# A store issued ahead of two transposing transfers of the same tile, on one queue (a four-layer graph network)

## The chip, the cores and the metric

One core of a Trainium2 chip. The metric is the device time of one execution in microseconds (us); most executions of a kernel agree within 0.3%.

## The reference, cut to what is computed

Nodes `x` (6250 x 128, float32), 206,250 edges sorted by target, and four layers, each fed with `relu(layernorm(x))` and added to `x`:

```python
h = relu(layernorm(x))
x = x + segment_sum(edge_weight[:, None] * (sigmoid(h @ W_gate + b_gate) * (h @ W0))[dst], src)   # layer 0
h = relu(layernorm(x))
x = x + segment_sum(h[src], dst) @ W1.T + b1                                                       # layer 1
# layer 2: messages from [h[src], h[dst]], summed by target, with a linear update
# layer 3: a hypergraph layer: sums over edges by one end, scaled by 1/degree, then by the other end,
#          scaled, then a normalisation over all nodes and a relu
```

## The kernel before, in words

The sums over edges are done as matrix products. The nodes are cut into 49 tiles of 128 (`TILES`). A stage called the build makes, for each tile j of source nodes, three matrices of 128 x 6272 (49 blocks of 128 columns, float16, 1.6 MB each): the counts of edges, and the edge weights in a high and a low part. All three stand in `stage[:, b, 0..2]`, with b = j % 2: there are two such buffers.

In the build, per tile:

- VectorE makes one-hot codes (`hots`, lines 788 to 791), eight sets a tile, in two buffers, and adds finished sums to X (`add_four`, line 803).
- TensorE multiplies them into PSUM (`half_windows`, lines 531 to 533: 16 units a tile), takes the high part off the exact sum (`take_high`, line 514), and makes the sums of layer 0 for the tile two back (`sums`, `sum_four`, lines 506 to 508): behind each of the first seven one-hot sets of tile j come up to eight blocks of tile j - 2, 24 matmuls. These read `wt[:, b]`, the turned weights. Before the first of them (line 539) it waits for both turned halves of that tile.
- ScalarE copies PSUM into `stage`: counts and high part together (line 1033, 16 a tile), the low part two units later (line 1016, 16 a tile). At the first unit of tile j, behind a low part of the tile before, it waits for the store (line 1026) and for both transposes (line 1027) of tile j - 2, whose buffer it is going to write.
- SyncE's queue hands each tile on (`hand_on`, lines 325 to 339). It waits until the sums of tile j - 2 are made (329) and until the tile's counts and high parts are copied (332, `hi_done`), loads half of the tile's rows for the sums (`g_in`, 333, 32 KB), issues the transposing transfer of the high part from `stage` to `wt` (334); then the same for the low part; then it stores the counts to DRAM (`by_source`, 336). Tile 0 also stores a filler (339).

`tiles_loop` unrolls seven tiles and then loops seven times over six tiles. After the build four phases read the counts back: phases 1 to 3 as they are (`a_pairs`, 366), phase 4 turned (`a_turned`, 356), and multiply them with the nodes' features (line 578). Before phase 1 all stores must have landed (`counts_stored`), and all additions be made (343).

Of the kernel before, what the change touches and what calls it, by code (L numbers as in the profile page):

```python
# [19 lines left out]
P = 128  # L20
NODES, EDGES = 6250, 206250
TILES = -(-NODES // P)
# [40 lines left out]
def slab(t, j):  # L63

    if isinstance(j, int):
        return t[j]
    return t[bass.ds(j, 1)].rearrange("a p n -> (a p) n")
# [7 lines left out]
def later(j, n):  # L75

    return not isinstance(j, int) or j >= n
# [46 lines left out]
def gnn_kernel(nc, x, src, dst, edge_weight, w0, wg0, bg0, w1, b1, wm, bm, wu, bu, hyper, w3, b3, gamma, beta, out):  # L124
    ctx = ExitStack()
    with ctx:
        sems = {}

        def s(name):
            if name not in sems:  # L130
                sems[name] = ctx.enter_context(nc.semaphore(name))
            return sems[name]
# [3 lines left out]
        def at(name, shape, dt, offset):  # L136
            size = int(np.prod(shape[1:])) * ESIZE[dt]
            return nc.alloc_sbuf_tensor_at(name, shape, dt, offset=offset), offset + -(-size // 32) * 32

        def keep(name, shape, dt):  # L140
            t, place[0] = at(name, shape, dt, place[0])
            return t
# [6 lines left out]
        by_source = nc.dram_tensor("counts_by_source", (TILES, P, (TILES + 1) * P), F16).ap()  # L149
# [14 lines left out]
        cols = keep("cols", [P, 8], F32)  # L164
# [22 lines left out]
        stage, o = at("stage", [P, 2, 1 + WEIGHTS, TILES, P], F16, o)  # L187
# [73 lines left out]
        def vec(ap):  # L261
            return ap.rearrange("(a b) -> a b", a=1)
# [23 lines left out]
        @block.sync  # L286
        def _(sp):

            for a, b in ((dst, dst_pad), (src, src_pad), (edge_weight.bitcast(I32), w_pad)):
                sp.dma_start(b[0:EDGES].rearrange("(a b) -> a b", a=15), a.rearrange("(a b) -> a b", a=15)).then_inc(s("pad_in"), 16)  # L290
            sp.wait_ge(s("pads"), 2)
            for k, b in ((1, dst_pad), (0, src_pad), (0, w_pad)):
                sp.dma_start(vec(b[EDGES:PADDED]), pad_rows[0:1, k, :]).then_inc(s("pad_in"), 16)

            sp.dma_start(X[:, 0:TILES - 1, :], x[0:(TILES - 1) * P].rearrange("(i p) f -> p i f", p=P)).then_inc(s("x_in"), 16)
            sp.wait_ge(s("x_zero"), 1)
            sp.dma_start(X[0:LAST, TILES - 1, :], x[(TILES - 1) * P:NODES]).then_inc(s("x_in"), 16)

            for to, of in ((w0g[:, 0:P], w0), (w0g[:, P:P + 1], wg0), (w3s[:], w3), (w_h[:, 0], wu[0:P]),
                           (wraw[:, 0], w1), (wraw[:, 1], wm[0:P]), (wraw[:, 2], wm[P:2 * P]), (wraw[:, 3], wu[P:2 * P]),  # L300
                           (b1s[:], spread(b1, P)), (bus[:], spread(bu, P)), (cols[:, 4:5], spread(bg0, 1)),
                           (cols[:, 0:1], bm.rearrange("(a b) -> a b", b=1)), (cols[:, 1:2], b3.rearrange("(a b) -> a b", b=1)),
                           (cols[:, 2:3], gamma.rearrange("(a b) -> a b", b=1)), (cols[:, 3:4], beta.rearrange("(a b) -> a b", b=1))):
                sp.dma_start(to, of).then_inc(s("weights_in"), 16)
            sp.wait_ge(s("x_zero"), 2)
            sp.dma_start(hrows[0:TILES - 1, :], hyper[0:(TILES - 1) * P].rearrange("(i p) -> i p", p=P)).then_inc(s("weights_in"), 16)
            sp.dma_start(hrows[TILES - 1:TILES, 0:LAST], vec(hyper[(TILES - 1) * P:NODES])).then_inc(s("weights_in"), 16)

            sp.wait_ge(s("pad_in"), 96)
            sp.dma_start(dst_run[:], bass.AP(dst_pad.tensor, 0, [[RUN, P], [1, RUN + 1]])).then_inc(s("dst_in"), 16)  # L310
            sp.dma_start(w_run[:], bass.AP(w_pad.tensor, 0, [[RUN, P], [1, RUN]])).then_inc(s("w_in"), 16)
            for k, b in enumerate((src_pad, dst_pad, w_pad)):
                sp.dma_start(table[:, k * P:(k + 1) * P], bass.AP(b.tensor, 0, [[ALIGN, ROWS], [1, P]])).then_inc(s("table_in"), 16)  # L313

            def layers(general):
                if general:
                    for ph in range(5):
                        general_sum(ph)
                    return

                sp.wait_ge(s("g_parts"), SET)
                sp.dma_start(g_dram.rearrange("i p n -> p i n"), G[:].rearrange("p i a f -> p i (a f)")).then_inc(s("g_stored"), 16)
                sp.wait_ge(s("g_stored"), 16)

                def hand_on(j, k, c):

                    b = c % 2
                    if later(j, 2):
                        sp.wait_ge(s("four_done"), (j - 1) * FOURS)
                    for a, done in enumerate(("hi_done", "lo_done")):  # L330
                        part = slice(a * P, (a + 1) * P)
                        sp.wait_ge(s(done), (j + 1) * HALVES)
                        sp.dma_start(g_in[:, b, part], slab(g_dram, j)[:, part]).then_inc(s(f"g_loaded{b}"), 16)
                        sp.dma_start_transpose(wt[:, b, a], stage[:, b, 1 + a].rearrange("p i d -> p (i d)")).then_inc(s(f"wt_in{b}"), 16)  # L334
                    cols = slice(j * P, (j + 1) * P) if isinstance(j, int) else bass.ds(j * P, P)
                    sp.dma_start(by_source.rearrange("i p n -> p i n")[:, :, cols], stage[:, b, 0]).then_inc(s(f"stored{b}"), 16)
                    if isinstance(j, int) and j == 0:

                        sp.dma_start(by_source.rearrange("i p n -> p i n")[:, :, TILES * P:], stage[:, b, 0]).then_inc(s("filled"), 16)

                tiles_loop(sp, hand_on, 0)
                counts_stored(sp)
                sp.wait_ge(s("added"), FOURS * TILES)

                for ph in (1, 2, 3, 4):

                    def step(j, k, c, ph=ph):
                        if not on(j):
                            return
                        if ph == 4:  # L350
                            if later(j, SLOTS):

                                sp.wait_ge(s("sum_done4"), j - (SLOTS - 1))
                            else:
                                sp.wait_ge(s("sum_done3"), min(TILES, 46 + c // 2 * 2))
                            sp.dma_start_transpose(a_turned[:, c % SLOTS], slab(by_source, j)[:, 0:TILES * P]).then_inc(s(f"turned_in{c % SLOTS}"), 16)  # L356
                        elif c % 2 == 0:
                            if later(j, SLOTS):

                                sp.wait_ge(s(f"sum_done{ph}"), j - (SLOTS - 2))  # L360
                            elif ph > 1:
                                sp.wait_ge(s(f"sum_done{ph - 1}"), min(TILES, 46 + c))
                            q = pair_at(ph, c) % 3
                            rows = by_source.rearrange("i p n -> p i n")
                            cols = slice(j * P, (j + 2) * P) if isinstance(j, int) else bass.ds(j * P, 2 * P)
                            sp.dma_start(a_pairs[:, q].rearrange("p i a d -> p i (a d)"), rows[:, :, cols]).then_inc(s(f"a_in{q}"), 16)

                    tiles_loop(sp, step, 0)

            def general_sum(ph):  # L370

                sp.wait_ge(s("g_rows_all"), ph + 1)
                sp.dma_start(h_dram.rearrange("(i p) f -> p i f", p=P), rows_all[:]).then_inc(s("g_table"), 16)
                with sp.Fori(0, CHUNKS) as c:
                    sp.wait_ge(s("g_free"), c + (ph * (CHUNKS + 1) + 1))
                    for a, b in enumerate((src_pad, dst_pad, w_pad)):
                        sp.dma_start(edge_in[:, a:a + 1], b[bass.ds(c * P, P)].rearrange("(a b) -> a b", b=1)).then_inc(s("g_in"), 16)

            branch(sp, layers)

            for g in range(6):
                sp.wait_ge(s("x_out"), 8 * (g + 1))
                sp.dma_start(out[g * 8 * P:(g + 1) * 8 * P].rearrange("(i p) f -> p i f", p=P), X[:, g * 8:(g + 1) * 8, :]).then_inc(s("out_stored"), 16)
            sp.wait_ge(s("x_out"), TILES)
            sp.dma_start(out[(TILES - 1) * P:NODES], X[0:LAST, TILES - 1, :]).then_inc(s("out_stored"), 16)
            sp.wait_ge(s("out_stored"), 16 * 7)
# [744 lines left out]
```

## Time and profile before

| | us |
|---|---|
| median of 3 runs | 2862.77 |
| lowest, highest | 2861.38, 2884.23 |
| the profiled execution | 2846.73 |
| its span, first to last instruction | 2844.9 |
| mean granted TensorE clock | 0.954 |

The profile is of one execution. "SPq" is SyncE's queue: an issue of a transfer has there the time in which it holds the queue, which isn't the time to its landing. "Idle before" of a group is put down to what ended the idle time. The clock is a share of the full 2.4 GHz. Landing is counted from the start of the issue.

### The profile page before, as it was taken

Reading aid. Unit: us, or ns where it says so; the run is one execution under the profiler, and the core shown is the slowest. Engines: PE = TensorE matmul, PEld = TensorE weight load, DVE = VectorE, ACT = ScalarE, POOL = GpSimd, SP = SyncE. Lnnn points to the kernel's source line nnn. Section 1 sums busy time; section 2 is a strip of 40 time slices with the busy share of each in tenths; the row PEclk is TensorE's granted clock in tenths of the full one; section 3 lists DMA queues with packets and bytes.
Section 4 is the critical chain, followed back from the end, with each engine's and each line's share of the span. In section 5 each row is a group of like instructions: output and inputs, shape, how many; then the busy total and the mean of one; then the engine's idle time right before and its main releaser. Section 6 shows DMA issues by size and latency. Waiting matters only on the chain.

```text
span 2844.9 us, 72345 instructions
## 1 busy us (share of the span) xinstructions
PE 2373.2 (83%) x27975; PEld 2024.3 (71%) x27975; DVE 1614.5 (57%) x3456; ACT 1214.5 (43%) x2626; POOL 66.4 (2%) x59
## 2 busy tenths in 40 slices
PE   1626898888888888898893999869997799999996
PEld 0414777777776777777772888758886688888884
DVE  5387998898898988898985111232223222212114
ACT  0605777776776777776773000141112211111113
POOL 0430000000000000000000000000000000000000
PEclk9999999999999999999996999979999899999997
DMA  9615999999999999999997999959999699999995
GB/s 280 181 45 114 195 198 196 193 186 195 188 189 188 196 178 200 181 203 193 183 204 185 264 278 274 280 150 251 258 250 257 167 289 291 283 240 252 252 252 121
DMA packets 1784416, 603.26 MB, mean 212 GB/s; under 512 B 1258086, under 2 KB 1781098, under 8 KB 1784093
## 3 DMA queue, kind: packets, MB, share of 16 engines
q1 hardware_dynamic: 1782538, 594.63, 97.8%
q0 software_dynamic: 1600, 4.92, 0.6%
q8 instruction: 176, 2.88, 0.4%
q14 instruction: 102, 0.84, 0.1%
HBM read 276.78 MB, written 109.03 MB: 136 GB/s over the span
## 4 chain that ended last, share of the span: by engine, by line
PE 43%; SPq 21%; DVE 10%; DMA 9%; issue 9%; ACT 6%; DVEq 1%; POOL 1%; ACTq 0%; POOLq 0%
PE ps L578 30%; SPq L334 10%; SPq L356 9%; DMA counts_by_source<-stage 7%; DVE X L803 4%; PE ps L506 3%; PE ps L508 2%; PE ps L507 2%; ACT hbig L992 2%; DMA edge_table<-w_pad 2%; DVE hot_c L791 2%; ACT stage L1033 2%; ACT stage L1016 1%; PE ps L531 1%; SPq L313 1%
## 5 line engine op out<-in xcount | busy, mean ns | idle before, releaser
L578 PE MATMUL ps<-Ha,a_pairs 128*128 128x258 f16 x7203 | 827.0, 275 | 103.6 <-ACT Ha L1061 103.6
L578 PEld LDWEIGHTS ps<-Ha,a_pairs 128*128 128x128 f16 x7203 | 705.3, 98 | 214.8 <-ACT Ha L1061 104.3
L1033 ACT CAST stage<-ps 128x784 f16<-128x784 f32 x784 | 653.5, 834 | 221.3 <-DMA counts_by_source<-stage 98.8
L531 PE MATMUL ps<-hot_c,hot_r 128*128 128x98 f16 x3136 | 517.1, 214 | 11.6 <-DVE hot_c L791 7.4
L532 PE MATMUL ps<-hot_c,hot_r 128*128 128x98 f16 x3136 | 511.7, 213 | 0.0
L533 PE MATMUL ps<-hot_c,hot_r 128*128 128x98 f16 x3136 | 510.7, 213 | 0.0
L1016 ACT CAST stage<-ps 128x392 f16<-128x392 f32 x784 | 396.5, 506 | 208.0 <-PE ps L514 207.9
L506 PE MATMUL ps<-g_in,wt 128*128 128x128 f16 x2401 | 438.5, 225 | 45.4 <-DVE X L803 32.6
L1072 ACT COPY extra<-ps 128x2 f32 (+1 forms) x196 | 31.4, 160 | 1037.9 <-PE ps L578 1037.9
L507 PE MATMUL ps<-g_in,wt 128*128 128x128 f16 x2401 | 435.0, 224 | 0.0
L508 PE MATMUL ps<-g_in,wt 128*128 128x128 f16 x2401 | 434.0, 223 | 0.0
L803 DVE SCALAR_TENSOR_TENSOR X<-ps,X 128x512 f32<-128x512 f32 (+1 forms) x637 | 394.0, 659 | 16.8 <-PE ps L508 15.6
L791 DVE TENSOR_TENSOR hot_c<-hot_c,meta_w 128x1568 f16<-128x1568 f16 x392 | 382.4, 976 | 0.0
L531 PEld LDWEIGHTS ps<-hot_c,hot_r 128*128 128x128 f16 x3136 | 311.5, 99 | 86.7 <-ACT stage L1016 41.8
L514 PE MATMUL ps<-stage,minus 128*128 128x392 f16 x784 | 265.6, 339 | 125.6 <-ACT stage L1033 72.1
L532 PEld LDWEIGHTS ps<-hot_c,hot_r 128*128 128x128 f16 x3136 | 314.1, 100 | 20.7 <-issue 1.6
L533 PEld LDWEIGHTS ps<-hot_c,hot_r 128*128 128x128 f16 x3136 | 314.0, 100 | 0.0
L506 PEld LDWEIGHTS ps<-g_in,wt 128*128 128x128 f16 x2401 | 240.4, 100 | 84.9 <-DVE X L803 74.0
L788 DVE TENSOR_TENSOR hot_c<-iota_c,meta 128x784 f16<-128x784 f16 x392 | 221.9, 566 | 135.7 <-PE ps L533 109.1
L578 PE MATMUL ps<-Hb,a_turned 128*128 128x258 f16 x2401 | 278.0, 274 | 18.7 <-DMA a_turned<-counts_by_source 15.6
L901 DVE TENSOR_TENSOR agg<-ps,low 128x128 f32<-128x128 f32 x98 | 28.6, 292 | 433.4 <-ACT low L1075 433.4
L578 PEld LDWEIGHTS ps<-Hb,a_turned 128*128 128x128 f16 x2401 | 231.9, 98 | 59.6 <-DMA a_turned<-counts_by_source 15.7
(176 smaller groups left out, 2083.3 us busy)
## 6 DMA issues: line engine op xcount, KB each, us to landing
a_pairs<-counts_by_source SPq DMA_DIRECT2D x75, 3136.0 KB, 14.0
counts_by_source<-stage SPq DMA_DIRECT2D x50, 1568.0 KB, 9.6
edge_table<-src_pad SPq DMA_DIRECT2D x1, 6464.0 KB, 27.9
edge_table<-dst_pad SPq DMA_DIRECT2D x1, 6464.0 KB, 49.5
edge_table<-w_pad SPq DMA_DIRECT2D x1, 6464.0 KB, 48.0
gated_parts<-G SPq DMA_DIRECT2D x1, 3136.0 KB, 12.6
g_in<-gated_parts SPq DMA_DIRECT2D x98, 32.0 KB, 3.3
out_x<-X SPq DMA_DIRECT2D x6, 512.0 KB
```

Source lines behind the costliest of these rows:

```text
L334: sp.dma_start_transpose(wt[:, b, a], stage[:, b, 1 + a].rearrange("p i d -> p (i d)")).then_inc(s(f"wt_in{b}"), 16)
L506: mm(o, wt[:, b, 0, i], g_in[:, b, 0:P], start=i % 4 == 0, stop=False, skip_group_check=True)
L507: mm(o, wt[:, b, 0, i], g_in[:, b, P:2 * P], start=False, stop=False, skip_group_check=True)
L508: last = mm(o, wt[:, b, 1, i], g_in[:, b, 0:P], start=False, stop=True, skip_group_check=True)
L531: mm(into(0), rows_, codes(0), start=v == 0, stop=True, skip_group_check=True)
L532: mm(into(1), rows_, codes(1), start=v == 0, stop=False, skip_group_check=True)
L533: last = mm(into(1), rows_, codes(2), start=False, stop=True, skip_group_check=True)
L578: last = mm(ps[:, c % 2, 0:PARTS], a_slot(ph, c, i), moving[:, i], start=i == 0, stop=i == TILES - 1)
L791: v.tensor_tensor(hot_c[:, b, :, 1:1 + WEIGHTS], hot_c[:, b, :, 0].unsqueeze(2).to_broadcast([P, PAIRS, WEIGHTS, WCOLS, 2]), meta_w[:, pai ...
L803: v.scalar_tensor_tensor(xs, ps[:, 6 + e, 0:(hi - lo) * P], 1.0 / (W_UP * H_UP), xs, ALU.mult, ALU.add).then_inc(s("added"), 1)
L1016: a.copy(stage[:, b, 2, :, u * SET_COLS:(u + 1) * SET_COLS], of).then_inc(s("lo_done"), 1)
L1033: a.copy(stage[:, b, 0:2, :, u * SET_COLS:(u + 1) * SET_COLS], of).then_inc(s("hi_done"), 1)
```

## The change

The store of the counts (and tile 0's filler) moves, from behind both transposes, to between the first small load and the first transpose. Its condition, `hi_done` of the whole tile, holds there already. Waits, sizes and semaphores stay.

```diff
+                def store_counts(j, b):
+
+                    cols = slice(j * P, (j + 1) * P) if isinstance(j, int) else bass.ds(j * P, P)
+                    sp.dma_start(by_source.rearrange("i p n -> p i n")[:, :, cols], stage[:, b, 0]).then_inc(s(f"stored{b}"), 16)
+                    if isinstance(j, int) and j == 0:
+
+                        sp.dma_start(by_source.rearrange("i p n -> p i n")[:, :, TILES * P:], stage[:, b, 0]).then_inc(s("filled"), 16)
+
                 def hand_on(j, k, c):
...
                         sp.wait_ge(s(done), (j + 1) * HALVES)
                         sp.dma_start(g_in[:, b, part], slab(g_dram, j)[:, part]).then_inc(s(f"g_loaded{b}"), 16)
+                        if a == 0:
+                            store_counts(j, b)
                         sp.dma_start_transpose(wt[:, b, a], stage[:, b, 1 + a].rearrange("p i d -> p (i d)")).then_inc(s(f"wt_in{b}"), 16)
-                    cols = slice(j * P, (j + 1) * P) if isinstance(j, int) else bass.ds(j * P, P)
-                    sp.dma_start(by_source.rearrange("i p n -> p i n")[:, :, cols], stage[:, b, 0]).then_inc(s(f"stored{b}"), 16)
-                    if isinstance(j, int) and j == 0:
-
-                        sp.dma_start(by_source.rearrange("i p n -> p i n")[:, :, TILES * P:], stage[:, b, 0]).then_inc(s("filled"), 16)
```

## Rows read from the trace of the kernel before

**Rows 1.** The page: the chain that ended last, by engine and by line.

```profile
PE ps L578 30%; SPq L334 10%; SPq L356 9%; DMA counts_by_source<-stage 7%; DVE X L803 4%; PE ps L506 3%; PE ps L508 2%; PE ps L507 2%; ACT hbig L992 2%; DMA edge_table<-w_pad 2%; DVE hot_c L791 2%; ACT stage L1033 2%; ACT stage L1016 1%; PE ps L531 1%; SPq L313 1%
```

**Rows 2.** Waits of the build, 228 to 1515: us in total, times, longest.

```profile
ACT stage L1033 <- DMA counts_by_source<-stage: 98.8, 23, 15.7
...
PE ps L506 <- DMA wt<-stage: 9.6, 2, 8.5
```

**Rows 3.** SyncE's queue in order of time, 1040 to 1075: start, us held.

```profile
1050.37 0.34 SPq L333 DMA_DIRECT2D g_in<-gated_parts  x1
1050.76 8.28 SPq L334 DMA_TRANSPOSE wt<-stage  x1
...
1059.70 8.64 SPq L334 DMA_TRANSPOSE wt<-stage  x1
1068.52 1.01 SPq L336 DMA_DIRECT2D counts_by_source<-stage  x1
1073.47 2.84 SPq L333 DMA_DIRECT2D g_in<-gated_parts  x1
```

**Rows 4.** The chain of waits: tile 0, then 1045 to 1110 (start, us, what).

```profile
261.77 16.27 DMA counts_by_source<-stage
...
1068.52 10.83 DMA counts_by_source<-stage
...
1083.17 0.11 PE ps L506
...
1102.27 0.33 SPq L333
```

**Rows 5.** Line 334: ns on the queue; us to landing (minimum, median, maximum).

```profile
L334 SPq DMA_TRANSPOSE wt<-stage x98: 7337/7922/8987, 244.9 to 1493.6; - x98
...
DMA to landing us min/median/max: 9.3/11.0/12.2
```

**Rows 6.** Line 336: the store's time to landing.

```profile
DMA to landing us min/median/max: 8.8/9.6/11.3
```

**Rows 7.** SyncE's queue in order of time, 260 to 277 (tile 0, then tile 1).

```profile
261.14 0.59 SPq L336 DMA_DIRECT2D counts_by_source<-stage  x1
261.77 7.16 SPq L339 DMA_DIRECT2D counts_by_source<-stage  x1
268.97 7.33 SPq L333 DMA_DIRECT2D g_in<-gated_parts  x1
```

**Rows 8.** Line 334 in 1076 to 1085: landing of the tile that followed.

```profile
L334 SPq DMA_TRANSPOSE wt<-stage x2: 7480/7764/8048, 1076.4 to 1084.5; - x2
...
DMA to landing us min/median/max: 9.3/9.6/9.9
```

**Rows 9.** Stretches: us, busy by engine, clock, DMA share, GB/s (last column).

```profile
1053.00:1059.70 6.70, 6.48 (x112) 5.67 (x110) 6.70 (x11) 5.21 (x10) 0.00 (x0) 1.00 1.17 219
1059.70:1061.30 1.60, 1.43 (x26) 1.28 (x26) 1.60 (x4) 1.60 (x3) 0.00 (x0) 1.00 1.23 34
```

**Rows 10.** TensorE in order of time, 1072 to 1086.

```profile
1074.34 0.22 PE L506 MATMUL ps<-g_in,wt 128*128 128x128 f16 x1
...
1075.62 0.22 PE L508 MATMUL ps<-g_in,wt 128*128 128x128 f16 x1
1080.31 0.34 PE L514 MATMUL ps<-stage,minus 128*128 128x392 f16 x1 [4.47 <-ACT stage L1033]
```

**Rows 11.** The stretch behind the stall, columns as in rows 9.

```profile
1080.00:1084.00 4.00, 3.64 (x36) 3.25 (x37) 0.66 (x2) 3.75 (x7) 0.00 (x0) 0.58 1.22 256
```

**Rows 12.** SyncE's queue in order of time, 1459 to 1517 (last two hand-ons).

```profile
1460.58 0.33 SPq L333 DMA_DIRECT2D g_in<-gated_parts  x1
...
1484.45 0.35 SPq L333 DMA_DIRECT2D g_in<-gated_parts  x1
```

**Rows 13.** The chain of waits, 1480 to 1530.

```profile
1493.60 9.45 DMA wt<-stage
...
1515.43 9.57 DVE stats L834 x49
```

## The prediction

> **What bounds the kernel now.** I read the page first, for where the end is set. Half of the span is the four later sums (line 578). The build, from about 228 to 1515 us, is what the change touches, and in the chain of waits it appears as SyncE's queue issuing transposes (L334, 10%) and as the store's own transfer (counts_by_source<-stage, 7%) [rows 1]. So in part of the build the three transfers of a tile stand on the path, one after another.
>
> Second, the waits of the build: ScalarE's first copy into `stage` (L1033) waits 98.8 us in 23 pieces for the store, mean 4.3 us, while TensorE waits for `wt` only twice [rows 2]. ScalarE's wait at the head of a tile is for three things of the tile two back: its store and its two transposes. The store is the latest of them, because it is issued last.
>
> Third, SyncE in order of time over one tile [rows 3]. Its hand-on begins at 1050.37; the first transpose is issued 0.39 later and holds the queue 8.28 us, the second begins at 1059.70 (0.66 after the first ends) and holds it 8.64, the store is issued at 1068.52 and is off the queue in 1.01 us. By the chain it lands 10.83 us later, at 1079.35 [rows 4]. From hand-on to landing that is 28.98 us. The next tile's copies end at about 1073.3 (its hand-on is at 1073.47), 23.1 us after this one's: that is a tile without a wait. The hand-on after that is at 1102.27 [rows 4]. So the pair repeats: 29.0 us of transfers, then a tile of 22.8 us, 51.9 us for two tiles of 23.1. Only every second tile stalls, because the stall itself gives the other chain time.
>
> **What the change does to this chain.** No instruction is added or removed. Store, first transpose, second transpose take the place of first, second, store. All three must land before ScalarE goes on, so the question is whether the sum of the three is shorter in the new order.
>
> The old sum by medians: 0.4 (first small load) + 7.92 (first transpose on the queue) + 0.66 + 7.92 + 0.2 + 9.6 (store to landing) = 26.7 us [rows 3, 5, 6]; the stalled tile in front of us had 28.98.
>
> The new one hangs on what the store does to the next instruction of the queue. It looks cheap (0.45 to 1.01 us), but the traces show its cost on its successor. In tile 0 two stores follow one another: the first is issued at 261.14, the second is held 7.16 us, to 268.93, and the small load behind the second is held 7.33 us, to 276.30 [rows 7]. In the loop the small load of the next tile, issued 4.95 us behind the store, is held 2.84 us (0.34 otherwise), to 7.8 us after the store's issue [rows 3]. So whatever follows a store is released 7.4 to 7.8 us after the store's issue; I take 7.5. Today the next tile pays little for it, since it comes 5 us later anyway. In the new order the first transpose stands right behind the store and pays all of it: the store is no 0.45 us in front of the transposes, it is 7.5 us.
>
> New sum: 0.5 to the store's issue + 7.5 + 7.92 + 0.66 = the second transpose is issued 16.6 us after the hand-on, against 9.0 before; it lands 11.0 later by the median of all, 9.3 to 9.9 in a tile whose hand-on found a store still moving [rows 5, 8]. Like against like: by medians 0.5 + 7.5 + 7.92 + 0.66 + 11.0 = 27.6 against 26.7, +0.9 us; with the slow first transpose of the stalled tile (8.28) 27.9 against its 28.98, -1.1. The best that a row allows is 0.5 + 7.5 + 7.5 + 0.66 + 9.9 = 26.1 against 28.98, -2.9. I take -0.2, near the middle of the first two. In the stalled tiles, of which I count 20 of the 23 (some are 0.5 us long), that is 20 x -0.2 = -4 us; the ends are -58 and +18.
>
> What could make it much shorter is the use of the DMA engines. Between the first and the second transfer there is a hole of 1.6 us in which they move 34 GB/s instead of 219, and a like one between second and third [rows 9]; a transfer of 1.6 MB is 7.3 us at 219 GB/s. The new order closes at most one hole: the first transpose's descriptors may be in the making while the store's last data move.
>
> **The cover that is lost.** TensorE's sums for the tile two back need `wt`. Today the transposes land some 8 us before the store, so TensorE does the first 24 matmuls of these sums while ScalarE stands: from 1074.34 to 1075.7, 1.33 us, and VectorE adds them; then it is idle 4.47 us until ScalarE is back [rows 10]. In the new order `wt` lands last, so ScalarE and these sums are released at the same moment. TensorE starts 0.87 us earlier than now (1079.44 against 1080.31), but with 1.33 us of work in front: +0.46 us at full clock. It comes back from the idle time at the lower clock (1.2 GHz): the next sums stand on the chain with 0.11 us a matmul (one of 24 shown) where the others went at one each 0.055 us [rows 4, 10]. If the added 24 run wholly at that rate and nothing is won back, they cost 24 x 0.11 - 0.87 = 1.7 us. The granted clock is 0.58 in the 4 us after the stall [rows 11] and is 1.00 while the engine works on [rows 9]; it comes back some 4 us after work resumes, in either order, so I take 0.5: 20 x 0.5 = +10 us, with ends +9 and +34. Behind it VectorE's additions and one-hots are released later, and VectorE is what a tile without a wait runs on, so I see no slack that swallows it.
>
> **The end of the build.** Here nothing follows, and the old order was right: the last tile's second transpose lands at 1503.05, 18.6 us after the hand-on, TensorE waits 8.5 us for it, and sums and additions run to 1515.43 [rows 2, 12, 13]. The store lands behind them at no cost. In the new order the second transpose lands 26.1 to 27.6 after the hand-on: +7.5 to +9.0 us, and the hand-on itself is up to 1 us later, since the tile before keeps the queue 24.8 us (0.5 + 7.5 + 7.92 + 0.66 + 8.1) and hand-ons are 23.9 apart there (1460.58, 1484.45 [rows 12]). I take +9. The counts are needed by the next stage only after 1515, so the earlier store buys nothing.
>
> **At nothing.** In tiles that don't stall, the queue is free again 24.7 us after the hand-on instead of store + 7.5 = 24.8 to 25.9: the same. The other chain of the pair starts there as before. TensorE's stalls for its own instructions at the loop's return are before its wait for `wt` and stay, except that the fetches travel on the same DMA engines. The second store of tile 0 now holds the transposes too: the second of these lands 0.5 + 7.5 + 7.4 + 7.9 + 0.7 + 10 = 34 us after the hand-on; today the second store is issued 17.7 us after it and lands 16.3 later [rows 4, 7], 34 us too, and ScalarE waits for it. No loss.
>
> Sum: -4 + 10 + 9 = +15 us on the profiled execution, which took 2846.7 us (span 2844.9). The median of the three runs is 2862.8, 16 us above it; 2862.8 + 15 = 2878 us.
>
> Two rules of the Trainium skill bear on it (DMA: Bandwidth & Descriptors). In "SWDGE vs HWDGE vs iDMA" it calls the hardware's descriptor generation dedicated logic with a faster setup; read as "issuing is free", it would give the first rival below. The 7.16 and 7.33 us above speak against that reading. In "Queues, rings and completion order" it says that each engine takes the descriptors of a ring in ring order. By that the transposes queue behind the store's data wherever the queue itself lets them in: the three exchange places, and the last lands where the last did.
>
> **Rivals.** (a) The transpose isn't held behind a store (only a copy behind a copy is), and its descriptors pile up behind the store's. Then the engines never starve: 2.6 us to the first data (1050.4 to 1053), 3 x 7.3 = 21.9, some 0.5 to the landing, 25.0 us in all. Against 27.8, the mean of 26.7 and 28.98, the stalled tiles gain 2.8 us each, 20 x -2.8 = -56; cover +10, end +6.4: -40, 2823 us. For it: the hole in rows 9. Against it: rows 7, twice, on this queue. 0.14.
>
> (b) The other side: the transpose behind the store is held till the store has landed, not 7.5 us, because it is of another kind and uses the path of the engines in another mode. Place: between L336 and L334; price: 9.6 to 10.8 instead of 7.5 us. Chain 0.5 + 10.2 + 7.92 + 0.66 + 11.0 = 30.3, +2.5 us in 20 stalled tiles, the other chain then stalls too (queue 27.4 us per tile against 23.1), +10 cover, +12 end: about +75, 2938 us. It decides from some 8.5 us of hold on. For it: the time of a transpose to its landing spreads from 9.3 to 12.2 us with no copy in front of it at all [rows 5]. Against it: in rows 3 the small load was through at 1076.3, 3 us before the store landed, and the transpose behind it took only 7.48 us. 0.16.
>
> (c) The sums on the slow clock cost their whole 1.7 us, or more since the idle time before them is 1.3 us longer: -4 + 34 + 9 = +39, 2902 us. 0.2.
>
> My forecast, 2878 (its own range 2850 to 2900), 0.5. About 1% (28 us) is what a measurement of this kernel tells from no change. Faster by more: rival (a) and a little of the low end of the forecast, 0.17. Slower by more (above 2891): (b), (c) most of it, and the upper end of the forecast, 0.38. Within 1%: 0.45. Range for 8 in 10: 2825 to 2932, from a fraction of (a) to the foot of (b).
>
> **What would show it.** In the changed profile: ScalarE's L1033 waits for wt<-stage instead of counts_by_source<-stage, some 20 times, again 4 to 5 us; the first transpose stands on the queue 15 to 16 us instead of 7.9, the second 7.9 as before; the store's time to landing stays 9 to 10 us; the second transpose is issued 16.6 us after the hand-on and lands 26 to 28 after it. PE's L506 waits for wt<-stage in the stalled tiles too, and in the last tile about 17 us instead of 8.5. The pair of tiles takes 52 us or a little over. I am wrong if the first transpose is issued in 8 us (rival a), if it is held 18 us or more (rival b), or if the tile behind a stall is over 1 us longer than 22.7 (rival c).

## The result, and the profile after

The changed kernel takes 2882.5 us (median of 20 runs), the kernel before beside it 2872.1: ratio 1.0038, interval 1.0023 to 1.0053, +11 us. Forecast were +15 us (2878) and a time within 1%; the base of that forecast, 2862.8, was the median of three runs. One of the twenty runs of the changed kernel, at 3540 us and a granted clock of 0.67, is slow and isn't in the ratio.

The profiled execution of the changed kernel took 2890.4 us, 43.7 more than that of before. Most of this isn't the change's: its first hand-on comes at 268.3 us instead of 244.5, and nothing ahead of it was touched. A third profile of the kernel before has it at 267.8 and a span of 2871.2 us. The experiments ran on four chips: on one the first hand-on comes at 244.1 to 245.2 us, on the other three at 266.9 to 268.3, whichever kernel runs. So it goes with the chip, as far as these profiles show. Spans are therefore compared by stretches, and times by the ratios to the kernel before on the same chip.

The page of the changed kernel: span, and the chain by line.

```profile
span 2888.6 us, 72345 instructions
PE ps L582 30%; SPq L344 10%; SPq L360 9%; DMA wt<-stage 7%; DVE X L807 4%; PE ps L510 3%; PE ps L512 2%; PE ps L511 2%; ACT hbig L996 2%; DVE hot_c L795 2%; ACT stage L1037 1%; ACT stage L1020 1%; PE ps L518 1%; SPq L328 1%
```

The 7% that were the store's [rows 1] are now those of `wt<-stage`. Waits of the build, 228 to 1560 us (us in total, times, longest), against [rows 2]:

```profile
ACT stage L1037 <- DMA wt<-stage: 93.8, 24, 15.1
DVE X L807 <- PE ps L512: 89.4, 50, 13.7
PE ps L510 <- DMA wt<-stage: 89.4, 26, 14.3
```

ScalarE waits as often and nearly as long as before (98.8 us, 23 times), for the transposes instead of the store; TensorE, which waited for `wt` twice, now waits 26 times. SyncE's queue in order of time over one tile and the next (start, us held), against [rows 3]:

```profile
1153.07 0.34 SPq L341 DMA_DIRECT2D g_in<-gated_parts  x1
1153.59 0.41 SPq L328 DMA_DIRECT2D counts_by_source<-stage  x1
1154.04 14.49 SPq L344 DMA_TRANSPOSE wt<-stage  x1
1168.72 0.60 SPq L341 DMA_DIRECT2D g_in<-gated_parts  x1
1169.37 7.99 SPq L344 DMA_TRANSPOSE wt<-stage  x1
1179.07 0.34 SPq L341 DMA_DIRECT2D g_in<-gated_parts  x1
1179.59 0.41 SPq L328 DMA_DIRECT2D counts_by_source<-stage  x1
1180.04 14.63 SPq L344 DMA_TRANSPOSE wt<-stage  x1
```

The store is off the queue in 0.41 us and the transpose behind it stands 14.5 us where it stood 7.9: the hold of a store moved onto it. The second one is issued 16.3 us behind the hand-on. By the medians, 15.3 us pass from the store's issue to the end of the transpose's hold, of which 7.9 are the transpose's own [rows 5]: it is released after 7.4. The store on the queue, and its landing, against [rows 6]:

```profile
L328 SPq DMA_DIRECT2D counts_by_source<-stage x49: 406/407/1798, 268.7 to 1518.2; - x49
...
DMA to landing us min/median/max: 9.0/9.9/12.3
```

Taken hand-on by hand-on (49 of them, of which the two above are examples), the last of the three transfers lands 27.4 us behind the hand-on by the median, and 27.0 in a second profile of the changed kernel; three profiles of the kernel before give 27.7, 27.3 and 27.7.

The end of the build, in the chain of waits:

```profile
1517.70 0.34 SPq L341
...
1533.99 9.23 DMA wt<-stage
```

The last second transpose lands at 1543.22, 25.5 us behind its hand-on, against 18.6 [rows 12, 13]. From the last hand-on to VectorE's statistics, called the tail from here on, it is 38.2 us (31.0 before).

### The profile page after: what moved, and what is told of

Its sections match the earlier page's. It is cut to its first block, busy times and chain, and to the rows that moved or that the text cites. A ratio compares the mean times of both kernels' runs of the same rounds, so it can differ in the third digit from the quotient of the medians.

```text
span 2888.6 us, 72345 instructions
## 1 busy us (share of the span) xinstructions
PE 2379.5 (82%) x27975; PEld 2033.0 (70%) x27975; DVE 1619.1 (56%) x3456; ACT 1217.4 (42%) x2626; POOL 66.2 (2%) x59
## 4 chain that ended last, share of the span: by engine, by line
PE 43%; SPq 21%; DVE 12%; issue 8%; DMA 8%; ACT 6%; DVEq 1%; another core or an unknown queue 1%; ACTq 0%
PE ps L582 30%; SPq L344 10%; SPq L360 9%; DMA wt<-stage 7%; DVE X L807 4%; PE ps L510 3%; PE ps L512 2%; PE ps L511 2%; ACT hbig L996 2%; DVE hot_c L795 2%; ACT stage L1037 1%; ACT stage L1020 1%; PE ps L518 1%; SPq L328 1%
## 5 line engine op out<-in xcount | busy, mean ns | idle before, releaser
L510 PE MATMUL ps<-g_in,wt 128*128 128x128 f16 x2401 | 446.1, 227 | 126.6 <-DMA wt<-stage 89.4
L512 PE MATMUL ps<-g_in,wt 128*128 128x128 f16 x2401 | 443.5, 226 | 0.0
L511 PE MATMUL ps<-g_in,wt 128*128 128x128 f16 x2401 | 443.5, 226 | 0.0
L793 DVE TENSOR_TENSOR hot_r<-iota_r,meta 128x1024 f16<-128x1024 f16 x392 | 270.3, 690 | 0.0
## 6 DMA issues: line engine op xcount, KB each, us to landing
gated_parts<-G SPq DMA_DIRECT2D x1, 3136.0 KB, 12.5
```

The source lines that it names most:

```text
L510: mm(o, wt[:, b, 0, i], g_in[:, b, 0:P], start=i % 4 == 0, stop=False, skip_group_check=True)
L511: mm(o, wt[:, b, 0, i], g_in[:, b, P:2 * P], start=False, stop=False, skip_group_check=True)
L512: last = mm(o, wt[:, b, 1, i], g_in[:, b, 0:P], start=False, stop=True, skip_group_check=True)
```

## The experiments

All ratios are to the kernel before, beside which each ran.

**e0 and e12, the kernel before again.**

> The kernel before, once more, for what varies from one execution to the next. From the first hand-on to the last 1240 us (1239.97 in the profile of before), within 3 us. The first hand-on itself came at 244.5 in the profile of before and at 268.3 in that of the changed kernel, ahead of everything that the change touches: if that is chance, it comes anywhere between 240 and 270 here.

> The kernel before, a third profile, for the spread of its build: from the first hand-on to the last 1232 to 1240 us, tail 31 to 32, transfers 27.3 to 27.7 us from hand-on to the store's landing (medians). First hand-on at 244 or at 268 as this chip has it.

From the first hand-on to the last: 1231.9 and 1241.7 us, with 1240.0 in the first profile; "within 3 us" was too narrow for e0. So the build varies by 10 us between executions of one program, and one profile can't carry a verdict on 10 us. The first hand-on came at 244.1 (e0) and 267.8 (e12).

**e1, the last tile in the old order.** For SyncE the last six tiles are unrolled, and tile 48 issues its store last.

```diff
-                        if a == 0:
+                        if a == 0 and not old:
                             store_counts(j, b)
...
+                    if old:
+                        store_counts(j, b)
```

> The changed kernel, with the last tile handed on in the old order. If the end of the build cost what the last tile's second transpose lands later (25.5 us behind its hand-on in the changed kernel against 18.6), this takes 7 us off the changed kernel's +11: ratio to before 1.001 to 1.002, and the last tile's second transpose lands 18 to 19 us behind its hand-on. If the 11 us are all in the stalled tiles of the loop, the ratio stays at 1.004.

1.0014 (1.0000 to 1.0028). The chain of waits has the landing and the statistics back where they were:

```profile
1492.16 9.66 DMA wt<-stage
1514.69 9.57 DVE stats L847 x49
```

The term of the end is confirmed: the ratio is 0.0024 below that of the changed kernel, 7 us, and the tail is 31.1 us. Some 4 us (0 to 8) are left for the other 48 tiles.

**e2 and e3, TensorE's sums one one-hot set later**, in the old and in the new order.

```diff
-                            sums(j - 2, c % 2, k * (SLOTS // 2) + c // 2, h)
+                            if h:
+                                sums(j - 2, c % 2, k * (SLOTS // 2) + c // 2, h - 1)
```

> The kernel before, with TensorE's sums one one-hot set later, so that they no longer run while ScalarE stands. If the lost cover is worth 0.5 us in each of some 20 stalled tiles, this costs 10 us: ratio 1.003 to 1.004, and the stalled tile takes 23.2 instead of 22.7 us. If TensorE has room for them anyway, the ratio is 1.000 within its interval.

> The changed kernel, with TensorE's sums one one-hot set later, so that they don't stand between the release of ScalarE and TensorE's next unit. If it was their place that made the tile behind a stall longer (23.2 to 24.1 us against 22.7), this wins 10 us back on the changed kernel: ratio to before 1.000 to 1.001. If the tile is longer for another reason (the clock, the transfers beside it), it stays at 1.004.

e2 gave 0.9940 (0.9921 to 0.9959): a win of 17 us where a loss or nothing was expected. e3 gave 1.0027 (1.0010 to 1.0043), hardly less than the changed kernel. Waits of e2 in the build:

```profile
DVE X L804 <- PE ps L508: 94.0, 64, 17.6
...
ACT stage L1034 <- DMA counts_by_source<-stage: 33.5, 22, 15.8
```

ScalarE's wait for the store is down from 98.8 to 33.5 us. A tile without such a wait, from its first copy of counts to its last, takes 22.84 us against 22.80 in the kernel before (medians): it isn't longer for having the sums in another place. The transfers land 26.1 us behind the hand-on instead of 27.7. With the sums one set later in both, the new order costs 0.0087, 25 us, of which 7 are the end (tail 38.4 against 31.0 us).

**e7 and e11, the cover alone.** e2 moved the sums and took them out of the stall; here they keep their place and wait for the store as well. e11 leaves the wait out for the last two tiles.

```diff
                         pe.wait_ge(s(f"wt_in{b}"), n * 32)
+                        if not (isinstance(t, int) and t >= TILES - 2):   # e11; e7 without this line
+                            pe.wait_ge(s(f"stored{b}"), n * 16)
```

> The kernel before, with one wait more: TensorE's first sums of a tile wait for the store as well, so that they can't run while ScalarE stands, and keep their place. Moving the sums did two things at once; this does the one. If the lost cover makes the tile behind a stall longer (23.3 us on the mean in the changed kernel against 22.5), the same lengthening shows here, 0.5 to 0.9 us in some 12 to 20 tiles, +8 to +16 us: ratio 1.003 to 1.006. If the tiles were longer because of the order of the transfers, they stay at 22.5 to 22.7 and the ratio at 1.000 to 1.001.

> The added wait of TensorE for the store, left out for the last two tiles, where it put the store's landing on the path (tail 40.0 us instead of 31.0 to 31.8). The end of the build is back at 31 to 32 us. If the wait wins time in the loop, as 0.9975 with a tail 9 us longer says, the ratio falls to 0.994 to 0.995. If the 0.9975 was chance and the lost cover costs what the longer tile suggests, the ratio is 1.000 to 1.003.

e7: 0.9975 (0.9959 to 0.9991), although its tail is 40.0 us. e11: 0.9957 (0.9937 to 0.9977), tail 32.3. ScalarE's waits in e7 and e11:

```profile
ACT stage L1034 <- DMA counts_by_source<-stage: 80.9, 25, 15.6
```

```profile
ACT stage L1035 <- DMA counts_by_source<-stage: 79.5, 23, 15.7
```

The tile behind a stall (from ScalarE's first copy of counts to its last, means over the loop behind stalls of more than 2 us) is longer in both, 23.5 and 23.1 us against 22.5 to 22.6 in the three profiles of before, as supposed. But the stalls are shorter (80 us against 87 to 99), the tile behind the loop's return takes 23.3 instead of 23.7 to 24.0, and by e11's ratio the sum is a gain of 12 us, not a loss of 10.

**e6, the store between the transposes.**

```diff
                         sp.dma_start_transpose(wt[:, b, a], stage[:, b, 1 + a].rearrange("p i d -> p (i d)")).then_inc(s(f"wt_in{b}"), 16)
+                        if a == 0:
+                            store_counts(j, b)
```

> The store between the two transposes. What follows the store is the small load of the second half, and that is held: 7.5 us instead of 0.4. First transpose 7.9 on the queue and landed 10 to 11 behind the hand-on, second issued 16.9 and landed 27 to 28 behind the hand-on: the same sum as in the changed kernel, the same wait for wt, ratio 1.002 to 1.006. If it matters which kind of transfer is behind the store, the second transpose lands otherwise.

0.9980 (0.9964 to 0.9997), better than expected and than the changed kernel. Its queue:

```profile
1011.89 0.34 SPq L341 DMA_DIRECT2D g_in<-gated_parts  x1
1012.27 7.72 SPq L342 DMA_TRANSPOSE wt<-stage  x1
1020.18 0.45 SPq L328 DMA_DIRECT2D counts_by_source<-stage  x1
1020.80 6.73 SPq L341 DMA_DIRECT2D g_in<-gated_parts  x1
1027.58 7.91 SPq L342 DMA_TRANSPOSE wt<-stage  x1
1035.82 0.34 SPq L341 DMA_DIRECT2D g_in<-gated_parts  x1
```

The small load takes the hold (6.73 us), as foretold. The second transpose is issued 15.7 us behind the hand-on and the queue is free at 23.6; the medians are 16.1 and 24.1, where the changed kernel has 16.5 and 24.5. The last landing comes at 26.9 us by the median, the tail is 36.6. `wt` lands last here too:

```profile
ACT stage L1037 <- DMA wt<-stage: 83.9, 27, 14.5
```

So this run has the lost cover and nearly the late end of the changed kernel, and differs from it only in that the store stands behind the first transpose and not in front of it. That is worth 0.0058, 17 us, of which about 1 is the tail.

**e8, both edits together.**

> The two edits that came out below or at the kernel before, together: the store between the transposes (0.998) and the sums one set later (0.994 in the old order). If what the sums' place wins doesn't depend on the order of the transfers, the ratio is 0.992 to 0.994, the best so far. If the late landing of the second transpose takes it back, as in the changed kernel with later sums (1.0027), the ratio is 0.997 to 1.001.

0.9962 (0.9948 to 0.9976): between the two cases, and no better than e2 (0.9940). It isn't the win of later sums that shrinks. Later sums do two things: they leave the stall, as in e11, and they go to another place. In e6 and in the changed kernel they have left the stall already. What the other place adds is 0.0017 in the old order (e2 against e11), 0.0018 between the transposes (e8 against e6) and 0.0011 in the new order (e3 against the changed kernel): the same, within intervals of some 0.002.

**e10, the changed kernel again.**

> The changed kernel once more beside these, for a second profile of it: first transpose 14.5 us on the queue, second landed 27 to 28 us behind the hand-on, last one 25.5, tiles behind a stall 23.0 to 23.5 us; ratio 1.002 to 1.005.

1.0043 (1.0029 to 1.0057); first transpose 14.6 us, last landing 27.0, last tile 25.4, tail 37.3, tiles behind a stall 23.1 us: as expected.

**e4, the store from ScalarE's queue.**

```diff
+                    act.wait_ge(s("hi_done"), (j + 1) * HALVES)
+                    store_counts(j, b)      # with act.dma_start; taken out of SyncE's hand_on
```

> The store is issued from ScalarE's queue, behind the last copy of its tile; SyncE's queue has the two transposes alone. If a store holds only what is behind it on its own queue, the first transpose stands 7.9 us on the queue again instead of 14.6; the three share the engines, so that all have landed 24 to 26 us behind the hand-on instead of 27.5. Then the stalls shrink by 2 to 3 us in 20 tiles: ratio to before 0.98 to 0.99. If the hold comes from the DMA engines being busy with the store, the first transpose is held 14 to 15 us as in the changed kernel, and the ratio is 1.00 or above.

1.0146 (1.0118 to 1.0174), and the expectation that led to it fell. ScalarE's queue, then SyncE's, in order of time:

```profile
1027.13 0.38 ACTq L1015 DMA_DIRECT2D counts_by_source<-stage  x1
```

```profile
1027.47 0.34 SPq L333 DMA_DIRECT2D g_in<-gated_parts  x1
1027.85 15.66 SPq L334 DMA_TRANSPOSE wt<-stage  x1
1043.69 0.44 SPq L333 DMA_DIRECT2D g_in<-gated_parts  x1
1044.18 8.02 SPq L334 DMA_TRANSPOSE wt<-stage  x1
```

No store stands on SyncE's queue, and the transpose is held all the same, 15.7 us. So the hold isn't a matter of one queue's order; the two queues share what holds. The last landing is at 26.7 us behind the hand-on by the median, no later than in the changed kernel. What else makes the 42 us is seen in part in ScalarE's waits in the build:

```profile
ACT stage L1010 <- issue: 30.8, 6, 9.1
```

"issue" is time in which an engine waited for nothing that the profile shows. ScalarE has none of it in the kernel before. Five of the six pieces, 22 us, stand at returns of the loop, right behind a wait of the same kind on TensorE, and the tiles there take 26.9 us instead of 23.7 to 24.0. The tail (37.8 us) adds 6 to 7. No run tells what ScalarE waited for.

**e5, the counts stored in long rows.** Rows of 12.5 KB a partition instead of blocks of 256 B; the counts stand in DRAM in another order, so the later sums go over other edges.

```diff
-                    sp.dma_start(by_source.rearrange("i p n -> p i n")[:, :, cols], stage[:, b, 0]).then_inc(s(f"stored{b}"), 16)
+                    sp.dma_start(slab(by_source, j)[:, 0:TILES * P], stage[:, b, 0].rearrange("p i d -> p (i d)")).then_inc(s(f"stored{b}"), 16)
```

> The changed kernel, with the counts stored as rows of 12.5 KB a partition instead of blocks of 256 B: the same bytes, a 49th of the runs. The counts stand in DRAM in another order, so the later sums are over other edges; their time is the same. If the hold behind a store is the making of its descriptors, it falls from 7.5 to below 1.5 us, the first transpose stands under 10 us on the queue; the data take the engines 4 to 7 us still, and all have landed 20 to 25 us behind the hand-on: the build loses its stalls, ratio 0.97 to 0.985. If the hold goes by the bytes that the engines move, the first transpose stays at 12 to 15 us and the ratio above 0.99.

0.9753 (0.9726 to 0.9779). Its queue in order of time, and the page's issues with the store's time to landing (median, us):

```profile
969.37 0.36 SPq L327 DMA_DIRECT2D counts_by_source<-stage  x1
969.77 12.00 SPq L343 DMA_TRANSPOSE wt<-stage  x1
```

```profile
counts_by_source<-stage SPq DMA_DIRECT2D x50, 1568.0 KB, 6.9
```

The transpose stands 12.0 us, by the median 11.6: neither expectation in full. By the medians from the store's issue to the end of the hold, 12.5 us here and 15.3 in the changed kernel, less the 7.9 us of the transpose's own, it is released after 4.6 and 7.4 us, and the store lands at 6.9 and 9.9. The release comes 2.3 and 2.5 us ahead of the landing. In these two kernels the hold goes with the store's landing and not with the number of runs alone, which fell to a 49th; that it ends when the engines have taken the store's data is argued from this. The last transpose lands 23.9 us behind the hand-on instead of 27.4, the waits of ScalarE for `wt` are down to 26.0 us in 17. From the first hand-on to the last it is 1163.6 us against 1231.9 to 1241.7, so the 71 us by which the kernel is faster than before are won in the build and not in the later sums.

## Why the prediction was right, and where its terms were not

*The hold.* Right, and it decided the case. "Whatever follows a store is released 7.4 to 7.8 us after the store's issue": 7.4 here by the median (7.0 in the rows shown), transposes 14.5 us on the queue (15 to 16 foretold), the second issued at 16.3 to 16.5 us (16.6). The one sense in which the picture was too narrow is e4: it isn't SyncE's queue that is held but what both queues feed. Rival (a), no hold, is excluded; so is rival (b), a hold till the landing. Rival (c), whose sign was a tile behind a stall over 1 us longer than 22.7, is out as well: it takes 23.2 and 23.1 us.

*The chain.* Foretold -0.2 us from hand-on to the last landing; 27.7, 27.3, 27.7 became 27.4 and 27.0, about -0.4. The reading of the Trainium skill's rule on ring order (DMA: Bandwidth & Descriptors, "Queues, rings and completion order"), that the three exchange places and the last lands where the last did, agrees with these numbers.

*The end.* +9 foretold, 7 measured by e1, and 7.2 and 6.3 by the tails of the two profiles. TensorE's last wait for `wt` is 12.1 us, where about 17 were foretold.

*The lost cover.* This step failed: "20 x 0.5 = +10 us", with "no slack that swallows it". The tile behind a stall did grow, from 22.5 or 22.6 to 23.2 and 23.1 us. Its price was wrong in sign: e11, which does this and nothing else to the loop, is 12 us faster (0.0043 of 2871 us; 7 to 18 us by the interval). In its profile ScalarE's stalls are 14 us shorter than the mean of the three profiles of before, and what its tiles take beside the stalls is the same in total.

*At nothing.* This failed too, and in the other direction. "The queue is free again 24.7 us after the hand-on instead of store + 7.5 = 24.8 to 25.9: the same." The queue is free at that time. But before, the next hand-on began at 23.1 us, was held for a moment in its small load, and had its first transpose started by then. Now the hand-on itself begins only at 24.9, and the store stands in front of that transpose. What this costs is seen when the cover is taken from every order. Ratios to the kernel before, with the tails:

| | store last | store between | store first |
|---|---|---|---|
| sums out of the stall | 0.9957 (e11), 32.3 us | 0.9980 (e6), 36.6 | 1.0038 (the changed kernel), 38.2 |
| sums one set later | 0.9940 (e2), 31.0 | 0.9962 (e8), 37.1 | 1.0027 (e3), 38.4 |

From "last" to "first" it is 0.0081 and 0.0087, 23 and 25 us, of which 6 and 7 are the tail: 16 to 18 in the loop. From "last" to "between" it is 0.0023 and 0.0022, some 6 us, of which 4 and 6 are the tail. So the price in the loop isn't that of `wt` landing last, which "between" has too; it is that of the store in front of the first transpose. I had -4 for it, together with the chain.

The sum of +15 against +11 is therefore right partly by luck: two terms, -12 instead of +10 and +16 instead of -4, are off in opposite ways. How the 16 us come about is read from profiles and not shown by a run of its own. From an odd tile's hand-on to the landing of the next, even tile (means of 21 pairs, from tile 7 on) it is 51.9 and 51.8 us in the changed kernel and 50.9 in e6; it is 51.5, 50.7 and 50.9 before and 51.2 and 51.0 in e7 and e11. Of the 0.9 and 1.0 us against e6, 0.7 are the even tile's later hand-on, 25.1 us behind the odd one's instead of 24.3. The spread of the kernel before is as large as the difference, so the ratios carry this point. Open too is why the stalls are shorter when the sums leave them: the transfers take 26.1 us in e2 and 27.0 and 27.1 in e11 and e7, against 27.3 to 27.7, and no run tells more.

A slip in the working changes nothing: tile 0's second store was issued 17.3 us after the hand-on (261.77 [rows 7], the hand-on being at 244.48), not 17.7, and landed at 33.6. In the changed kernel tile 0's second transpose lands at 33.1 us, and "no loss" is right.

## What to carry to other kernels

Count a transfer at what it does to the next one issued, not at the time in which it is off its queue: here 0.4 us on paper were 7 us for whoever stood behind. When three transfers gate one buffer, exchanging them moves the gate; here the last landing stays within 1 us and the worst place for the store is in front of both transposes. What wins is less data time (long rows, 0.975, if the later stages can read that order) or a consumer that asks later (e2, 0.994, which beats both kernels of this case). And work that fills a stall isn't free: take it out once and measure, before a price is put on losing it.

## What the runs showed of the hardware that I had not expected

- A store issued from ScalarE's queue holds a transpose on SyncE's queue as long as one on its own: 15.7 us on the queue in the row shown (median 15.1) instead of 7.9.
- The transposes can move faster than the rate at which I took them. Stretches of the changed kernel, columns as in rows 9:

```profile
1024.20:1031.50 7.30, 7.24 (x126) 6.56 (x124) 7.02 (x13) 6.36 (x11) 0.00 (x0) 1.00 1.04 218
...
1035.00:1039.00 4.00, 3.84 (x69) 3.37 (x67) 4.00 (x7) 3.17 (x6) 0.00 (x0) 1.00 1.27 289
...
1042.00:1049.00 7.00, 2.57 (x38) 1.78 (x35) 3.03 (x5) 3.82 (x7) 0.00 (x0) 0.81 1.12 221
```

  The first is the store, at 218 GB/s; the second four us of the first transpose, at 289; the third seven us of the second, 221 on the mean, with 1 us at 100 GB/s in it and others at 291 and 295. In the kernel before, the transpose shown went at 219 [rows 9], and the one behind the stall at 256 [rows 11]. A mean rate doesn't tell whether the engines were kept waiting.
- Long rows shorten a store of 1.6 MB from 9.9 to 6.9 us to its landing, and 49 of them with what hangs on them are worth 2.5% of the kernel.
